# First attention: value products of two steps in one block behind a pair's denominators, with five probability slots and seven key slots

## The chip, the core and the metric

The kernel runs on one core of a Trainium2 chip. The core has five engines, each with its own queue, tied by semaphores only: TensorE (PE) multiplies matrices and writes into PSUM, VectorE (DVE) and ScalarE (ACT) read PSUM and work elementwise, GpSimd (POOL) works on SBUF alone, and SyncE (SP) issues most of the transfers. The metric is the device time of one execution in microseconds (us). Lower is better. All times here are for the whole program, of which the changed part is one stage.

## What is computed

The reference is a network of two layers on one sequence of 2048 tokens with 512 features, all in float32. Each layer has attention and a feed-forward part, with a residual and a layer norm behind each. The change touches the first attention alone:

```python
S, H, Dh = 2048, 16, 32
q = concat([x @ Wq_sem.T, rope(x @ Wq_geo.T)])    # 16 heads of 32
k = concat([x @ Wk_sem.T, rope(x @ Wk_geo.T)])
v = x @ Wv.T
scores = einsum('bhqd,bhkd->bhqk', q, k) / sqrt(32)
scores = where(causal, scores, float32.min)
attn = softmax(scores, axis=-1)
out = einsum('bhqk,bhkd->bhqd', attn, v)
x = layernorm(x + out @ Wo.T)
```

Behind it come a mixture of eight experts (two for each token) with a shared one, a second attention with 128-wide heads, and a gated feed-forward part with 2:4 sparsity. They aren't changed.

## The kernel before

**Items and steps.** The first attention (`layer0_attention`, from L478 on) works through 16 items: four chunks c of 512 queries (`CH`), and for each four groups g of four heads (`GH`). An item's keys are taken in tiles of 128; one step is one item with one key tile. Chunk c has 4c full tiles and four on the diagonal, so the items have 4, 8, 12 and 16 steps, 160 in all. For c > 0 full and diagonal tiles alternate as long as there are diagonal ones, then the remaining full ones follow. A diagonal step uses 512, 384, 256 or 128 of the queries. Two neighbouring steps are a pair; items have even numbers of steps, so no pair spans two items.

**What a step does.** For each of its four heads TensorE makes a *score* matmul (L726, 97 rows: 96 of split queries and keys and one that subtracts the row's maximum) into one of three banks `stb`, on the diagonal with a second one that adds the mask (L731). ScalarE makes the exponential of it (L619) into the step's slot of `probs`. Then follow the *value product* (`av`, L743: four matmuls, one for each head, with 32 columns of the array each, side by side, summed in `avb` over the item) and, once for each pair, the *denominators* (`den`, L759: four matmuls of the same shape with ones, summed in `den`). For the denominators GpSimd adds the second step's probabilities onto the first's, in place, in two halves of two heads (L590), and it may only do so when the value product of the first step is done. At the end of an item ScalarE copies `avb` (L633), VectorE turns the denominators and inverts them (L664, L668, L673: transpose, reciprocal, transpose), and GpSimd multiplies both into `X` (L600).

**The maxima.** The maximum that a score subtracts comes from a pass of its own, ahead of the item: *units* (L705), matmuls of queries with keys of up to 512 columns, into one of three banks `sbank`; VectorE takes the maximum of each (L645, on the diagonal L650), and at the item's end a *turn* (L657, L712, L626, L538, L540) brings the row of maxima to the queries. 640 units lie between the scores, about four for each step.

**What sets the order.** `attention0_plan` (L377 to L475) writes one list of events, and every engine goes through this same list in its own loop and picks its events: TensorE units, scores, `av` and `den`; GpSimd at an even `av` the pair's add (and, for the first 39 pairs, a transfer of zeros), and at the `den` of an item's last pair the multiply into `X`; VectorE at that `den` its three operations. `av` of step i-1 stands ahead of the last head's score of step i, and at odd i `den` of the pair i-3 stands behind it. Each engine's queue is worked off in this order, so whatever stands behind a waiting instruction waits too.

**Slots.** `probs` has four slots (`PSLOTS`), one a step: ScalarE may write slot i%4 when `av` and, by parity, `den` or the add of step i-4 is done. Keys are in eight slots (`KSLOTS`, parts of the buffers `hi` and `lo`), queries in three; SyncE loads 40 key chunks of three transfers each (L528) and may overwrite a slot when the last score that reads it is done.

Of the kernel before, what the change touches and what calls it, by code (L numbers as in the profile page):

```python
# [126 lines left out]
KSLOTS, QSLOTS, PSLOTS = 8, 3, 4  # L127
# [3 lines left out]
def key_slots(hi, lo):  # L131
    return [a[:, i, :].rearrange("p (h n) -> p h n", h=GH) for i, a in
            ((2, hi), (2, lo), (0, hi), (0, lo), (1, hi), (1, lo), (3, hi), (3, lo))]
# [243 lines left out]
def attention0_plan():  # L377
# [87 lines left out]
    for i, (n, kt) in enumerate(steps):  # L465
        for h in range(4):
            if h == 3 and i > 0:
                order.append(("av", i - 1))
                if i >= 3 and i % 2:
                    order.append(("den", i - 3))  # L470
            order.append(("scores", i, h))
            order += in_gap[k]
            k += 1
    order += [("av", len(steps) - 1), ("den", len(steps) - 2)]
# [3 lines left out]
def layer0_attention(nc, stage_before, qk_dram, m_dram, xs_dram, V, X, hi, lo, qst, consts, early):  # L478
# [14 lines left out]
    with ExitStack() as ctx:  # L493
# [3 lines left out]
        probs = m.sb("probs", [P, PSLOTS, GH, CH])  # L497
# [71 lines left out]
        def _(pool):  # L569
# [10 lines left out]
            for ev in order:  # L580
                if ev[0] == "av" and ev[1] % 2 == 0:
# [3 lines left out]
                    for a in range(2):  # L585
                        hs = slice(2 * a, 2 * a + 2)
                        pool.wait_ge(s["exp_ok"], 4 * (i + 1) + 2 * a + 2)
                        if a == 0:
                            pool.wait_ge(s["av_ok"], i + 1)
                        nc.gpsimd.tensor_tensor(probs[:, i % PSLOTS, hs, w0:], probs[:, i % PSLOTS, hs, w0:],  # L590
                                                probs[:, (i + 1) % PSLOTS, hs, w0:], ALU.add)\
                            .then_inc(s["pair_ok"], 1)
# [12 lines left out]
        def _(act):  # L605
            for ev in order:
                if ev[0] == "scores":
# [5 lines left out]
                    if i >= PSLOTS and h == 0:  # L613
                        act.wait_ge(s["av_ok"], i - PSLOTS + 1)
                        if i % 2 == 0:
                            act.wait_ge(s["den_ok"], (i - PSLOTS) // 2 + 1)
                        else:
                            act.wait_ge(s["pair_ok"], 2 * ((i - PSLOTS) // 2 + 1))
                    nc.scalar.activation(probs[:, i % PSLOTS, h, w0:], stb[:, k % 3, w0:], ACT.Exp, scale=SCALE0)\  # L619
# [58 lines left out]
        def _(pe):  # L678
# [12 lines left out]
            for ev in order:  # L691
# [41 lines left out]
                elif ev[0] == "av":  # L733
# [8 lines left out]
                    for h in range(GH):  # L742
                        last = nc.tensor.matmul(avb[HD0 * h:HD0 * (h + 1), w0:],  # L743
                                                V[:, kt, g * P + h * HD0:g * P + (h + 1) * HD0],
                                                probs[:, i % PSLOTS, h, w0:], start=start, stop=stop,
                                                tile_position=(0, HD0 * h), skip_group_check=True)
                    last.then_inc(s["av_ok"], 1)
                elif ev[0] == "den":
# [9 lines left out]
                    for h in range(GH):  # L758
                        last = nc.tensor.matmul(den[HD0 * h:HD0 * (h + 1), w0:], ones[:], probs[:, i % PSLOTS, h, w0:],  # L759
# [1445 lines left out]
def build(nc, ins, out):  # L2205
# [9 lines left out]
    with ExitStack() as ctx:  # L2215
# [20 lines left out]
        with ExitStack() as ffn:  # L2236
# [7 lines left out]
            with ExitStack() as both:  # L2244
                hi = both.enter_context(nc.sbuf_tensor("hi0", [P, ND, S], F32R))
                lo = both.enter_context(nc.sbuf_tensor("lo0", [P, ND, S], F32R))
# [3 lines left out]
                consts = (hidden, ident, identr, maskr)  # L2250
                stage = layer0_qkv(nc, ins["xT"], ins["wqk0"], ins["wv0"], ins["rope0"], ins["masks"], ins["eye"],
                                   X, V, hi, lo, qst, consts, qk0_dram)
                stage = layer0_attention(nc, stage, qk0_dram, m_dram, xs_dram, V, X, hi, lo, qst, consts, early)
# [108 lines left out]
```

## Time and profile before

| what | us |
|---|---|
| median of three runs | 2433.03 |
| lowest, highest | 2430.97, 2436.6 |
| profiled execution, its own time | 2435.74 |
| its span, first to last instruction | 2433.9 |
| first attention in it, first unit to last denominators | about 165 to 790 |

The stages follow one another, so the slices of the profile can be assigned: of 40 slices of 61 us the first attention fills those from the third to the thirteenth. Over the whole span TensorE is busy 91% of the time (2216.2 us), VectorE 51%, ScalarE 30%, GpSimd 27%, and the granted TensorE clock is 0.954 of its full value on average. How to read rows: a time is the start in us from the span's start, the next number the duration; `128x512` is partitions by elements of a row; x8 are eight neighbouring records of one kind in one row (the eight records of one `av` or `den` in float32 are four matmuls); the bracket is the idle time ahead and what ended it.

### The profile page before, as it was taken

What the parts mean: (1) busy time and instruction counts of PE and PEld (TensorE: products, weight loads), DVE (VectorE), ACT (ScalarE), POOL (GpSimd) and SP (SyncE); (2) the same over time, 40 slices, a digit from 0 to 9 for tenths busy, and PEclk for the clock granted to TensorE, in tenths of its full rate; (3) what the DMA queues carried; (4) which work ended last, traced back from release to release, by engine and by line L of the source; (5) the groups of instructions that cost most, each with busy time, mean ns of one, the idle gap of its engine ahead of it and who ended that gap; (6) DMA issues with size and microseconds to landing.
All of it is one profiled execution on the core that took longest, in us unless ns stands there. A gap on an engine that the chain in (4) does not pass through costs nothing. (4 is left out here: it accounts for less than half of the span.)

```text
span 2433.9 us, 27331 instructions
## 1 busy us (share of the span) xinstructions
PE 2216.2 (91%) x10140; PEld 1523.5 (63%) x10140; DVE 1244.0 (51%) x2244; ACT 734.5 (30%) x1318; POOL 663.5 (27%) x446
## 2 busy tenths in 40 slices
PE   7977999999998779999977877999999999999996
PEld 5864555455553544444446666888887787878775
DVE  6864577776660552222248872322224555455656
ACT  3322455555556332111123321211113221112222
POOL 5342455555556005110034633000003021211200
PEclk9976799999999889999998998999999999999999
DMA  4464244333210523232233425000011010100001
GB/s 176 173 179 120 82 117 128 106 87 79 66 27 19 210 94 138 74 113 78 83 122 129 137 106 190 27 18 27 18 35 44 9 35 18 35 17 17 18 18 52
DMA packets 102058, 196.07 MB, mean 81 GB/s; under 512 B 10080, under 2 KB 27360, under 8 KB 100512
## 3 DMA queue, kind: packets, MB, share of 16 engines
q1 hardware_dynamic: 92832, 164.29, 22.0%
q0 software_dynamic: 8240, 27.01, 3.2%
q10 hardware_dynamic: 864, 3.15, 0.4%
q8 instruction: 77, 1.26, 0.2%
q14 instruction: 45, 0.37, 0.0%
HBM read 127.69 MB, written 66.72 MB: 80 GB/s over the span
## 5 line engine op out<-in xcount | busy, mean ns | idle before, releaser
L619 ACT ACTIVATE a_probs<-a_stb 128x512 f32<-128x512 f32 (+3 forms) x640 | 308.8, 535 | 283.7 <-PE a_stb L731 168.8
L590 POOL TENSOR_TENSOR a_probs<-a_probs 128x1024 f32<-128x1024 f32 (+3 forms) x160 | 281.6, 1773 | 290.1 <-PE a_avb L743 275.1
L645 DVE TENSOR_REDUCE a_mparts<-a_sbank 128x1 f32<-128x512 f32 x384 | 239.8, 683 | 99.8 <-PE a_sbank L705 99.6
L2050 POOL CAST m_wh<-wst 128x1024 fp32r<-128x1024 f32 x24 | 27.6, 1148 | 727.4 <-POOLq L1811 373.6
L56 PE MATMUL m_gu<-hi,m_wh 128*128 128x512 f32 x512 | 202.4, 395 | 14.9 <-DVE m_h L2116 13.0
L57 PE MATMUL m_gu<-lo,m_wh 128*128 128x512 f32 x512 | 201.2, 393 | 0.0
L58 PE MATMUL m_gu<-hi,m_wl 128*128 128x512 f32 x512 | 201.1, 393 | 0.0
L650 DVE CUSTOM_DVE_ANT_0 a_junk<-a_sbank,hidden 128x128 bf16<-128x128 f32 (+3 forms) x256 | 113.8, 488 | 83.4 <-PE a_sbank L705 81.5
L743 PE MATMUL a_avb<-a_probs,V 128*32 128x512 f32 (+3 forms) x1280 | 155.6, 559 | 0.7 <-ACT a_probs L619 0.7
L705 PE MATMUL a_sbank<-hi,q 96*128 96x512 f32 (+3 forms) x320 | 134.6, 450 | 21.3 <-PEq L152 11.5
L2116 DVE TENSOR_TENSOR m_h<-m_sg,m_gu 128x512 f32<-128x512 f32 x64 | 43.9, 686 | 206.2 <-ACT m_sg L2080 206.1
L705 PE MATMUL a_sbank<-lo,q 96*128 96x512 f32 (+3 forms) x320 | 120.4, 412 | 17.6 <-DMA q<-qk 11.2
L726 PE MATMUL a_stb<-q,hi 97*128 97x512 f32 (+3 forms) x320 | 133.1, 427 | 1.5 <-ACT a_probs L619 1.3
L56 PE MATMUL a_sc<-hi,q 128*128 128x512 f32 x256 | 106.7, 417 | 19.1 <-PEq L1364 14.4
L726 PE MATMUL a_stb<-q,lo 97*128 97x512 f32 (+3 forms) x320 | 121.8, 392 | 1.6 <-ACT a_probs L619 1.2
L56 PEld LDWEIGHTS m_gu<-hi,m_wh 128*128 128x128 f32 x512 | 97.1, 190 | 37.6 <-DVE m_h L2116 15.6
L1895 DVE TENSOR_TENSOR a_ptl<-a_tb,a_pth 128x512 fp32r<-128x512 f32 x64 | 44.1, 691 | 149.2 <-ACT a_pth L1867 149.2
L2080 ACT ACTIVATE m_sg<-m_gu 128x512 f32<-128x512 f32 x64 | 38.3, 598 | 271.7 <-PE m_gu L58 248.8
L1867 ACT ACTIVATE a_pth<-a_tb 128x512 fp32r<-128x512 f32 x64 | 38.2, 598 | 243.0 <-PE a_tb L1935 243.0
L58 PEld LDWEIGHTS m_gu<-hi,m_wl 128*128 128x128 f32 x512 | 97.3, 190 | 20.7
L57 PEld LDWEIGHTS m_gu<-lo,m_wh 128*128 128x128 f32 x512 | 97.4, 190 | 20.2
L726 PEld LDWEIGHTS a_stb<-q,hi 97*128 97x128 f32 x320 | 62.7, 198 | 68.2 <-ACT a_probs L619 33.9
(256 smaller groups left out, 4765.9 us busy)
## 6 DMA issues: line engine op xcount, KB each, us to landing
qk<-v_hl SPq DMA_DIRECT2D x32, 512.0 KB, 2.7
hi<-qk SPq DMA_DIRECT2D x60, 256.0 KB, 4.8
lo<-qk SPq DMA_DIRECT2D x60, 256.0 KB, 5.6
q<-qk SPq DMA_DIRECT2D x48, 256.0 KB, 5.3
wst<-in_w_mlp SPq DMA_DIRECT2D x24, 512.0 KB, 3.5
xs<-a_zeros POOLq DMA_DIRECT2D x39, 256.0 KB, 2.5
w<-xs SPq DMA_DIRECT2D x39, 256.0 KB, 2.8
ys<-e_rows_b SPq DMA_DIRECT2D x39, 256.0 KB, 2.0
```

The lines of the kernel that those rows point to most:

```text
L56: nc.tensor.matmul(out, wh, xh, start=start, stop=False, skip_group_check=True)
L57: nc.tensor.matmul(out, wh, xl, start=False, stop=False, skip_group_check=True)
L58: return nc.tensor.matmul(out, wl, xh, start=False, stop=stop, skip_group_check=True)
L590: nc.gpsimd.tensor_tensor(probs[:, i % PSLOTS, hs, w0:], probs[:, i % PSLOTS, hs, w0:], probs[:, (i + 1) % PSLOTS, hs, w0:], ALU.add)\
L619: nc.scalar.activation(probs[:, i % PSLOTS, h, w0:], stb[:, k % 3, w0:], ACT.Exp, scale=SCALE0)\
L645: nc.vector.reduce_max(to, sbank[:, b, :], AX).then_inc(s["unit_max"], 1)
L650: nc.vector.tensor_tensor_reduce(out=junk[:, k % 2, 0:w], in0=sbank[:, b, 0:w], in1=hidden[:, CH - w:CH], scale=1.0, scalar=BIG, op0=ALU.a ...
L705: nc.tensor.matmul(bank[:, 0:w], qst[0:96, n % QSLOTS, h, t * P:(t + 1) * P], kst[at % KSLOTS][0:96, h, 0:w], start=True, stop=True)\
L726: last = nc.tensor.matmul(stb[:, k % 3, w0:], kst[slot_of[n, kt // TC] % KSLOTS][0:97, h, kt % TC * P:(kt % TC + 1) * P], qst[0:97, n % QS ...
L743: last = nc.tensor.matmul(avb[HD0 * h:HD0 * (h + 1), w0:], V[:, kt, g * P + h * HD0:g * P + (h + 1) * HD0], probs[:, i % PSLOTS, h, w0:], ...
L1895: nc.vector.tensor_tensor(ptl[:, 4 * g:4 * g + 4, :].rearrange("p a b -> p (a b)"), tb[:, (g + 1) % 2, :], f32(pth[:, 4 * g:4 * g + 4, :]) ...
L2116: tt(h[:, r, :], sg[:], gu[:, r % 2, 1, :], ALU.mult).then_inc(s["h_ok"], 1)
```

## The change

The list of events is written in another order. At odd i nothing stands between the scores any more. At even i, ahead of the last head's score, stand: `den` of the pair i-4, `av` of i-2, `av` of i-1, in this order. The end of the list is `den`, `av`, `av`, `den`. Since a step's probabilities are needed for longer, there is a fifth slot: `several` has four and `spare` is placed on the memory of the eighth key slot, so `KSLOTS` is 7. The waits of ScalarE, which go by the parity of i - 4, go by that of i - 5. Nothing else is changed: as many matmuls, adds, exponentials and transfers as before, one memset fewer.

```diff
-KSLOTS, QSLOTS, PSLOTS = 8, 3, 4
+KSLOTS, QSLOTS, PSLOTS = 7, 3, 5
...
-            ((2, hi), (2, lo), (0, hi), (0, lo), (1, hi), (1, lo), (3, hi), (3, lo))]
+            ((2, hi), (2, lo), (0, hi), (0, lo), (1, hi), (1, lo), (3, hi))]
...
         for h in range(4):
-            if h == 3 and i > 0:
-                order.append(("av", i - 1))
-                if i >= 3 and i % 2:
-                    order.append(("den", i - 3))
+            if h == 3 and i > 0 and i % 2 == 0:
+                if i >= 4:
+                    order.append(("den", i - 4))
+                order += [("av", i - 2), ("av", i - 1)]
             order.append(("scores", i, h))
             order += in_gap[k]
             k += 1
-    order += [("av", len(steps) - 1), ("den", len(steps) - 2)]
+    n = len(steps)
+    order += [("den", n - 4), ("av", n - 2), ("av", n - 1), ("den", n - 2)]
...
-        probs = m.sb("probs", [P, PSLOTS, GH, CH])
+        several = m.sb("probs", [P, PSLOTS - 1, GH, CH])
+        probs = [several[:, i] for i in range(PSLOTS - 1)] + [spare[:]]
...
                     if i >= PSLOTS and h == 0:
                         act.wait_ge(s["av_ok"], i - PSLOTS + 1)
-                        if i % 2 == 0:
+                        if (i - PSLOTS) % 2 == 0:
                             act.wait_ge(s["den_ok"], (i - PSLOTS) // 2 + 1)
                         else:
                             act.wait_ge(s["pair_ok"], 2 * ((i - PSLOTS) // 2 + 1))
...
+                lo_at = (nc.sbuf_base + 31) // 32 * 32
...
+                spare = nc.alloc_sbuf_tensor_at("spare0", [P, GH, CH], F32, offset=lo_at + 4 * 3 * S)
```

On TensorE, at the end of the last item's narrow steps (around its eighth step; `a_stb` are scores, `a_avb` a value product, `a_den` denominators). Before:

```order
L726 MATMUL a_stb<-q,lo 128x512 x3
L743 MATMUL a_avb<-a_probs,V 32x128 x4
L726 MATMUL a_stb<-q,lo 128x512 x4
L743 MATMUL a_avb<-a_probs,V 32x512 x4
L759 MATMUL a_den<-a_probs,a_ones 32x512 x4
L726 MATMUL a_stb<-q,lo 128x512 x4
```

The same place now:

```order
L728 MATMUL a_stb<-q,hi 128x512 x3
L761 MATMUL a_den<-a_probs,a_ones 32x512 x4
L745 MATMUL a_avb<-a_probs,V 32x512 x4
L745 MATMUL a_avb<-a_probs,V 32x128 x4
L728 MATMUL a_stb<-q,hi 128x512 x8
```

The value products left their places between four scores each; two stand together, behind the denominators, and eight scores of 512 columns follow in a row.

On GpSimd, from the last narrow pair of the second last item to the first pairs of the last one (`a_probs<-a_probs` is a pair's add, x2 its halves; `X` the multiply). Before:

```order
L590 TENSOR_TENSOR a_probs<-a_probs 128x2x128 x2
L590 TENSOR_TENSOR a_probs<-a_probs 128x1024 x10
L600 TENSOR_TENSOR X<-a_avs,a_rt 128x512
L590 TENSOR_TENSOR a_probs<-a_probs 128x2x384 x2
```

The same place now:

```order
L592 TENSOR_TENSOR spare_57<-spare_57,a_probs 128x2x128 x2
L592 TENSOR_TENSOR a_probs<-a_probs 128x1024 x2
L592 TENSOR_TENSOR a_probs<-a_probs,spare_57 128x1024 x2
L592 TENSOR_TENSOR a_probs<-a_probs 128x1024 x4
L602 TENSOR_TENSOR X<-a_avs,a_rt 128x512
L592 TENSOR_TENSOR spare_57<-spare_57,a_probs 128x1024 x2
L592 TENSOR_TENSOR a_probs<-a_probs 128x2x384 x2
```

Between the narrow pair and the multiply stood five full adds (x10), now four; the fifth, the first of the new item, moved behind the multiply.

## Rows read from the trace of the kernel before

**Rows 1.** Windows, core 0: stretch, length, busy us of each engine, PEclk, DMA share, GB/s.

```profile
300.00:734.00 434.00, 422.49 (x2616) 223.74 (x2610) 303.39 (x705) 243.19 (x503) 242.35 (x161) 1.00 0.34 86
```

**Rows 2.** Waits of PE, 190 to 790 us: us in total, times, longest.

```profile
PE a_sbank L705 <- DVE a_mparts L645: 7.5, 18, 1.1
```

**Rows 3.** Timeline of PE and DVE, 601 to 605 us: start, us, engine, line, operation.

```profile
601.25 0.39 PE L705 MATMUL a_sbank<-hi,q 96*128 96x512 f32 x1
601.57 1.07 PE L743 MATMUL a_avb<-a_probs,V 128*32 128x512 f32 x8
602.45 1.04 PE L759 MATMUL a_den<-a_probs,a_ones 128*32 128x512 f32 x8
603.42 0.50 PE L726 MATMUL a_stb<-q,lo 97*128 97x512 f32 x1
603.76 0.40 PE L705 MATMUL a_sbank<-hi,q 96*128 96x512 f32 x1
603.99 0.40 PE L726 MATMUL a_stb<-q,lo 97*128 97x512 f32 x1
...
604.19 2.49 DVE L645 TENSOR_REDUCE a_mparts<-a_sbank 128x1 f32<-128x512 f32 x4 [1.43 <-PE a_sbank L705]
```

**Rows 4.** Timelines of PE and ACT, 733 to 790 us, without units in between.

```profile
733.96 1.06 PE L743 MATMUL a_avb<-a_probs,V 128*32 128x512 f32 x8
734.96 0.97 PE L726 MATMUL a_stb<-q,hi 97*128 97x512 f32 x3
...
767.02 0.98 PE L726 MATMUL a_stb<-q,lo 97*128 97x512 f32 x3
767.56 2.07 ACT L619 ACTIVATE a_probs<-a_stb 128x512 f32<-128x512 f32 x4 [1.41 <-PE a_stb L726]
768.21 0.50 PE L726 MATMUL a_stb<-q,lo 97*128 97x512 f32 x1 [0.21 <-ACT a_probs L619]
...
780.80 1.07 PE L743 MATMUL a_avb<-a_probs,V 128*32 128x512 f32 x8
...
789.37 1.07 PE L759 MATMUL a_den<-a_probs,a_ones 128*32 128x512 f32 x8 [1.86 <-POOL a_probs L590]
```

**Rows 5.** Timeline of PE, POOL and DVE around an item's final denominators, 688 to 693 us.

```profile
688.22 1.06 PE L743 MATMUL a_avb<-a_probs,V 128*32 128x512 f32 x8
689.11 1.04 PE L759 MATMUL a_den<-a_probs,a_ones 128*32 128x512 f32 x8
689.47 4.70 POOL L590 TENSOR_TENSOR a_probs<-a_probs 128x1024 f32<-128x1024 f32 x2 [2.60 <-PE a_avb L743]
690.21 0.72 DVE L664 STREAM_TRANSPOSE a_dt<-a_den 128x512 f32<-128x512 f32 x1 [1.14 <-PE a_den L759]
691.25 0.71 DVE L673 STREAM_TRANSPOSE a_rt<-a_rec 128x512 f32<-128x512 f32 x1
691.89 2.44 DVE L645 TENSOR_REDUCE a_mparts<-a_sbank 128x1 f32<-128x512 f32 x4
692.60 0.50 PE L705 MATMUL a_sbank<-lo,q 96*128 96x512 f32 x1 [0.50 <-DVE a_mparts L645]
```

**Rows 6.** Groups of POOL by form, 190 to 790 us: xcount, busy us, mean ns.

```profile
L590 POOL TENSOR_TENSOR a_probs<-a_probs 128x768 f32<-128x768 f32 x32 | 57.9, 1828 | 86.4 <-PE a_avb L743 86.2 <-ACT a_probs L619 0.2
L600 POOL TENSOR_TENSOR X<-a_avs,a_rt 128x512 f32<-128x512 f32 x15 | 19.3, 1290 | 0.2
```

**Rows 7.** Timeline of PE, 225 to 240 us.

```profile
231.27 9.55 PE L705 MATMUL a_sbank<-hi,q 96*128 96x512 f32 x16 [5.26 <-DMA q<-qk]
```

**Rows 8.** Later stage: two waits in PE's timeline, and the window behind the first.

```profile
1909.40 0.50 PE L56 MATMUL m_gu<-hi,m_wh 128*128 128x512 f32 x1 [2.73 <-DVE m_h L2116]
...
2045.67 0.50 PE L56 MATMUL m_gu<-hi,m_wh 128*128 128x512 f32 x1 [2.02 <-DVE m_h L2116]
...
1910.80:1914.20 3.40, 3.40 (x10) 2.66 (x9) 1.53 (x3) 0.00 (x0) 0.00 (x0) 0.52 0.00 0
```

**Rows 9.** Key loads of L528, from issue to landing.

```profile
DMA to landing us min/median/max: 3.2/4.9/8.6
```

More of the change, by code:

```diff
@@ L473, in attention0_plan, with layer0_attention @@
             k += 1
-    order += [("av", len(steps) - 1), ("den", len(steps) - 2)]
+    n = len(steps)
+    order += [("den", n - 4), ("av", n - 2), ("av", n - 1), ("den", n - 2)]
     return items, steps, first, final, units, loads, last_use, order
-def layer0_attention(nc, stage_before, qk_dram, m_dram, xs_dram, V, X, hi, lo, qst, consts, early):
+def layer0_attention(nc, stage_before, qk_dram, m_dram, xs_dram, V, X, hi, lo, qst, consts, early, spare):
     items, steps, first, final, units, loads, last_use, order = attention0_plan()
@@ L589, in _ @@
                             pool.wait_ge(s["av_ok"], i + 1)
-                        nc.gpsimd.tensor_tensor(probs[:, i % PSLOTS, hs, w0:], probs[:, i % PSLOTS, hs, w0:],
-                                                probs[:, (i + 1) % PSLOTS, hs, w0:], ALU.add)\
+                        nc.gpsimd.tensor_tensor(probs[i % PSLOTS][:, hs, w0:], probs[i % PSLOTS][:, hs, w0:],
+                                                probs[(i + 1) % PSLOTS][:, hs, w0:], ALU.add)\
                             .then_inc(s["pair_ok"], 1)
@@ L618, in _ @@
                             act.wait_ge(s["pair_ok"], 2 * ((i - PSLOTS) // 2 + 1))
-                    nc.scalar.activation(probs[:, i % PSLOTS, h, w0:], stb[:, k % 3, w0:], ACT.Exp, scale=SCALE0)\
+                    nc.scalar.activation(probs[i % PSLOTS][:, h, w0:], stb[:, k % 3, w0:], ACT.Exp, scale=SCALE0)\
                         .then_inc(s["exp_ok"], 1)
@@ L744, in _ @@
                                                 V[:, kt, g * P + h * HD0:g * P + (h + 1) * HD0],
-                                                probs[:, i % PSLOTS, h, w0:], start=start, stop=stop,
+                                                probs[i % PSLOTS][:, h, w0:], start=start, stop=stop,
                                                 tile_position=(0, HD0 * h), skip_group_check=True)
@@ L758, in _ @@
                     for h in range(GH):
-                        last = nc.tensor.matmul(den[HD0 * h:HD0 * (h + 1), w0:], ones[:], probs[:, i % PSLOTS, h, w0:],
+                        last = nc.tensor.matmul(den[HD0 * h:HD0 * (h + 1), w0:], ones[:], probs[i % PSLOTS][:, h, w0:],
                                                 start=start, stop=stop, tile_position=(0, HD0 * h),
@@ L2250, in build @@
                 consts = (hidden, ident, identr, maskr)
+                spare = nc.alloc_sbuf_tensor_at("spare0", [P, GH, CH], F32, offset=lo_at + 4 * 3 * S)
                 stage = layer0_qkv(nc, ins["xT"], ins["wqk0"], ins["wv0"], ins["rope0"], ins["masks"], ins["eye"],
                                    X, V, hi, lo, qst, consts, qk0_dram)
-                stage = layer0_attention(nc, stage, qk0_dram, m_dram, xs_dram, V, X, hi, lo, qst, consts, early)
+                stage = layer0_attention(nc, stage, qk0_dram, m_dram, xs_dram, V, X, hi, lo, qst, consts, early, spare)
             xt = V[:].rearrange("p (d c) n -> p d (c n)", d=ND)
```

## The prediction

> **What bounds the kernel now.** I read the windows first, to find the stage that the change touches and which engine is full in it. From 300 to 734 us TensorE is busy 97% of the time at a granted clock of 1.00, VectorE 70%, ScalarE 56%, GpSimd 56% [rows 1]. Then the table of waits of TensorE in this stage (190 to 790 us): the largest that recurs is 18 waits of 7.5 us in all, for VectorE's maxima [rows 2]. So the stage goes by TensorE's own sequence; a change there counts in full, and a new wait on TensorE counts in full too. Then the timeline of one pair of steps, for what the sequence costs. Value and denominator matmuls use 32 columns of the array at four tile positions, the others all 128. Two neighbours of the 32-column kind start 0.88 us apart, neighbours of the full kind 0.23. At a border it is more: 0.32 from the last full one to the value product, 0.34 from the first full one to the next, and 0.97 from the denominators to the first full one [rows 3]; 1.00 where a value product stands alone [rows 4]. So a value product that stands alone pays (0.32 - 0.23) + (1.00 - 0.88) + (0.34 - 0.23) = 0.32 us for its borders. Last, the timeline around a final denominator, for the chain that hangs on GpSimd [rows 5], whose durations are in the table by form [rows 6].
>
> **What the change removes.** 160 blocks of 32-column work become 80 (the order shows all of it: block, four heads' products, block). 80 borders of 0.32 us are 25.6 us. Nine of them lie in the last 55 us, which I sum apart, and some three before 231 us, where TensorE waits 5.26 us for a query load [rows 7] and gives nothing back. 68 x 0.32 = **-21.8 us**. VectorE's three small operations after a final denominator run now behind the first scores of the next stretch, where the third or fourth unit waits 0.50 us for them [rows 5]; they will run beside a block of 2.7 us. I take half of the 7.5 us of [rows 2]: **-4 us**.
>
> **What it adds: GpSimd before the block.** The pair's add of the block at T starts when that block's first value product is done, and must have ended when the next block starts, since that now begins with the pair's denominators. A value product starts and 1.25 us later the add does (688.22 to 689.47), which takes 4.70 us for two full halves [rows 5]. The denominators stand first, so the next block is at T + 0.88 + 1.25 + 4.70 + 0.05 = T + 6.9 at the earliest (0.05 as where a score follows the end of the exponential that it waits for, 767.56 + 0.60 and 768.21 [rows 4]). The pair of steps is three products of 0.88, a way out of 0.09 and a stretch of eight scores and seven or eight units, 3.9 to 4.2: 6.6 to 6.9. So plain pairs just fit, for **+1 us** in all. Before, the denominators came last in their block, 0.88 us later.
>
> **The final pairs don't fit.** In the order of GpSimd the multiply into X now stands ahead of the next item's first add (it was behind it). The multiply needs three VectorE operations on the denominators: the first starts 1.10 us after these (689.11 to 690.21), the last ends at 691.96, 2.85 after them [rows 5]. VectorE has its last units to finish at that point, so I add 0.2. The multiply takes 1.29 [rows 6]. Only then the add: T + 3.05 + 1.29 + 4.70 + 0.05 = **T + 9.1**. What TensorE has in these places is 6.85 (2.73 in the block, about 4.1 in the stretch, which has a diagonal step with its mask matmuls). So it stands still for 2.25 us, ahead of denominators that all the rest of its work is queued behind, scores and units included; ScalarE and VectorE run dry with it. There are 15 such places. One lies in the tail, two in the first 260 us are covered by the query load and by TensorE at half its clock. 12 x 2.25 = **+27 us**. The bounds: 1.7 us where the stretch has more in it, 2.6 where VectorE is later.
>
> **Longer stretches on three banks.** VectorE takes a full unit each 0.60 us (four in 2.49, the last 0.69) and starts 0.43 after the matmul [rows 3]; TensorE goes on 0.71 after the start of the maximum that it waits for (691.89 is the first, the wait ends at 692.60 [rows 5], and the bank is the one of three before). In a stretch of four units nothing waits. In one of eight, unit j starts at 0.34 + 0.467j unhindered, and can't before 1.48 + 0.60(j - 3): at j = 7 that is 3.88 against 3.61, 0.27 us late; with a ninth unit early in the stretch 0.63. Of some 15 such stretches ten are of the first kind or have mask matmuls between, five of the second: 10 x 0.3 + 5 x 0.63 = **+6 us** (3 to 9). ScalarE keeps up: one exponential per 0.49 us.
>
> **The tail.** Once the units are over (from 733.96), eight pairs of steps take 46.8 us until 780.80, and the last denominators start 8.57 later [rows 4]. The scores of a stretch are then paced by ScalarE: the fourth waits until the first exponential has ended (1.19 after the first score), the rest follow by 0.49 ((2.06 - 0.60)/3 of [rows 4]), so eight scores and the way into the block are 1.19 + 4 x 0.49 + 0.4 = 3.6, where two stretches of four took 3.2. By the chains: four plain full pairs at 6.9, one final at 9.1, and three with narrower diagonal steps: 5.8 (the add is two of 1.83 [rows 6]: 0.88 + 1.25 + 3.66), 5.0 by TensorE and 5.6 by ScalarE. That is 53.1, **+6.3 us**. At the end two full chains follow one another, 2 x 6.9 = 13.8 instead of 8.57, less the 2.06 us by which a block now starts earlier (a denominator and a value product that it no longer has behind it, and a border): **+3.2 us**.
>
> **The clock.** In the later stages, at full clock too, seven waits of TensorE of 1.9 to 2.7 us stand in the trace; after three of them the granted clock fell: behind one of 2.73 us the row shows 0.52 over 3.4 us, which is 1.2 of 2.4 GHz nearly throughout; after one of 2.02 us nothing fell [rows 8]. Each fall costs half of its length, 1.7 us. 13 waits of 2.25 us and more (the 12 and the tail's one) x 3/7 x 1.7 = **+9.5 us** (0 to 35, if the falls are longer and come at each). The Trainium skill ("TensorE: Matmul & The Clock Gate", "Why this matters for your kernels") only warns of pauses longer than the ones forecast here. By it this term would be nil; the rows say otherwise, and the rows decide.
>
> **Key slots, loads.** Seven slots instead of eight don't move a single unit or score in the order. The tightest load is freed ten scores ahead of its first use, with a block between: 10 x 0.47 + 2.7 = 7.4 us and more. Its three transfers are issued 0.43 apart and land 4.9 after that (median; 8.6 at most [rows 9]): about 6.2. Nothing, or some 2 us in one place. A memset less is nothing.
>
> **Sum** against the profiled execution's 2435.74: -21.8 - 4 + 1 + 27 + 6 + 6.3 + 3.2 + 9.5 = **+27.2 us**. The median of the runs shown is 2433.03, so **2460**.
>
> **Rivals.**
> - *No fall of the clock.* All as above without the last term: 2433 + 18 = 2451. For it: four of seven such waits left the clock alone. 0.27.
> - *The clock falls at each stall and in the tail*, where TensorE is then idle a third of each pair: 13 x 1.7 = 22 instead of 9.5, 8 more in the tail, where slower value products also delay the adds that hang on them, and some falls of twice the length: 2433 + 18 + 22 + 8 + 5 = 2486. 0.14.
> - *Faster: GpSimd isn't last.* If the add of the first pair didn't wait behind the multiply, the final pairs would be at 6.9 as well and TensorE's borders would be what is left: -21.8 - 4 + 1 + 6 + 2 = -17, 2416. It decides at T + 6.9: an add that ends before that costs nothing. Against it stands the order of GpSimd, in which the multiply comes first, and that the engine works in order. 0.08.
> - *Partly covered.* Stalls of 1 us less and short rings: -12 -3, so near +3 us, 2436. 0.07.
> - *Late keys.* The load of 6.2 us against 7.4 lands late at a dozen places by 1 us: 2472. 0.04.
> - *That it doesn't do what it says*: the blocks are halved in the order, but a value product next to another one might pay a load that one next to denominators doesn't. 80 x 0.2 more: 2476. 0.02.
> The forecast itself has 0.38.
>
> **The numbers.** Below 2440 lie the faster case and the partly covered one, 0.15; above 2490 a part of the clock's case. A range from 2438 to 2488 holds the rest. A measurement of this kernel can tell about 0.2%, 4.9 us, from no change. Faster: 0.08 and a third of the partly covered: 0.09. Within: 0.07. Slower: 0.84.
>
> **What the profile after would show.** Right: 80 blocks; the multiply into X ahead of an add; about 13 waits of TensorE for GpSimd's adds of about 2 us, each right after a final denominator's block and ahead of the next denominators, and short ones in the last 50 us; VectorE waits on its units about 0.3 us at the end of long stretches; the clock below 1.00 somewhere between 300 and 790. Wrong: if the table of waits has no such row the final pairs' term falls and the kernel is faster; if the borders inside a block are over 0.9 the first term does.

## The result, and the profile after

| | before | after |
|---|---|---|
| median of four runs, us | 2432.70 | 2452.05 |
| lowest to highest | 2430.97 to 2436.60 | 2448.17 to 2456.19 |
| span of the profiled execution | 2433.9 | 2454.4 |
| mean granted clock | 0.954 | 0.950 |
| last denominators of the first attention | 789.37 | 806.25 |

The changed kernel takes 1.0075 times as long (95% interval 1.0062 to 1.0089); the medians differ by 19.4 us. Of the 20.5 us between the two spans 16.9 stand at the last denominators. Nearly all of the other 3.6 came up in two steps of 1.6 us in the last stage of the network, which the change doesn't touch: 24.4 us at half clock there against 17.8. I count them as scatter, which was not tested. Of ten executions of the run `both`, further down, one took 3157.7 us at a mean granted clock of 0.648; its times here are those of the other nine.

Lines of functions are two higher in the kernel after: L707 are units, L728 scores, L745 value products, L761 denominators, L592 GpSimd's adds, L602 its multiply into X. The same window and the waits of TensorE (190 to 805 us), to be held against [rows 1, 2]:

```profile
300.00:734.00 434.00, 407.93 (x2519) 220.77 (x2518) 291.27 (x680) 236.17 (x486) 232.58 (x155) 0.97 0.33 85
...
PE a_den L761 <- POOL a_probs L592: 24.0, 17, 2.5
PE a_sbank L707 <- DMA q<-qk: 9.6, 3, 6.8
PE a_den L761 <- POOL spare L592: 8.6, 5, 3.1
PE a_sbank L707 <- DVE a_mparts L647: 3.8, 15, 0.3
```

TensorE's busy share fell from 97% to 94%, its clock from 1.00 to 0.97, and a row that was nearly absent (one wait of 1.9 us) is now the largest: 32.6 us of waits for GpSimd's adds in 22 places, and one of 4.0 at 806 us outside this window. The waits for maxima went down to half.

A fixed amount of work is the fairest comparison. From the sixth turn to the last one both kernels run 2641 matmul records of this stage. Windows of before and of after:

```profile
294.33:733.52 439.19, 427.36 (x2641) 226.12 (x2642) 307.70 (x712) 245.54 (x509) 243.76 (x163) 1.00 0.33 86
```

```profile
279.96:736.52 456.56, 427.77 (x2641) 231.01 (x2641) 304.51 (x712) 246.91 (x509) 245.90 (x165) 0.97 0.32 85
```

So the middle became 17.4 us longer. But the sixth turn comes 14.4 us *earlier* than before, which I had not forecast, and from the last turn to the last denominators it takes 69.7 us instead of 55.9. 16 matmul records, two products or 1.8 us, moved from before the sixth turn to behind the last one. Without them the start gained 12.6 us, the middle lost 17.4 and the tail 12.1: together the 16.9.

**A final pair after.** Timeline of PE, DVE and POOL in the tail, where nothing else covers the wait:

```profile
752.21 1.07 PE L761 MATMUL a_den<-a_probs,a_ones 128*32 128x512 f32 x8 [0.43 <-POOL a_probs L592]
...
753.35 0.72 DVE L666 STREAM_TRANSPOSE a_dt<-a_den 128x512 f32<-128x512 f32 x1 [16.88 <-PE a_den L761]
...
754.39 0.71 DVE L675 STREAM_TRANSPOSE a_rt<-a_rec 128x512 f32<-128x512 f32 x1
...
755.24 1.27 POOL L602 TENSOR_TENSOR X<-a_avs,a_rt 128x512 f32<-128x512 f32 x1 [3.08 <-DVE a_rt L675]
...
756.47 4.67 POOL L592 TENSOR_TENSOR spare<-spare,a_probs 128x1024 f32<-128x1024 f32 x2
...
761.20 1.08 PE L761 MATMUL a_den<-spare,a_ones 128*32 128x512 f32 x4 [3.06 <-POOL spare L592]
```

The next denominators start 761.20 - 752.21 = 8.99 us later, with the multiply ahead of the add. The forecast was T + 9.1. In the middle the same wait stands at each final pair, 0.7 to 2.4 us long: the largest are 2.31, 2.32 and 2.37 at 583, 642 and 702 us. During one of them, 0.9 us before it ends, the clock falls; the wait and a window that begins there:

```profile
641.98 1.93 PE L761 MATMUL a_den<-a_probs,a_ones 128*32 128x512 f32 x8 [2.32 <-POOL a_probs L592]
```

```profile
641.20:644.60 3.40, 2.62 (x16) 0.65 (x20) 0.00 (x0) 0.00 (x0) 0.73 (x1) 0.50 0.00 0
```

0.50 is 1.2 of 2.4 GHz. By windows of 0.5 us laid side by side TensorE is at this level for 30.6 us between 300 and 805 us; in the kernel before it never is between 300 us and its last denominators.

**The end.** The last two blocks of PE:

```profile
799.46 1.06 PE L761 MATMUL a_den<-a_probs,a_ones 128*32 128x512 f32 x8 [1.95 <-POOL a_probs L592]
...
806.25 1.94 PE L761 MATMUL a_den<-a_probs,a_ones 128*32 128x512 f32 x8 [4.01 <-POOL a_probs L592]
```

### The profile page after: what moved, and what is told of

It reads as the page before. It is cut to its first block and busy times, and to the rows that moved or that the text cites. A ratio compares the mean times of both kernels' runs of the same rounds, so it can differ in the third digit from the quotient of the medians.

```text
span 2454.4 us, 27325 instructions
## 1 busy us (share of the span) xinstructions
PE 2216.8 (90%) x10140; PEld 1530.7 (62%) x10140; DVE 1241.4 (51%) x2244; ACT 735.0 (30%) x1318; POOL 659.7 (27%) x445
## 3 DMA queue, kind: packets, MB, share of 16 engines
q1 hardware_dynamic: 92832, 164.29, 21.8%
## 5 line engine op out<-in xcount | busy, mean ns | idle before, releaser
L621 ACT ACTIVATE a_probs<-a_stb 128x512 f32<-128x512 f32 (+3 forms) x512 | 249.5, 538 | 202.3 <-PE a_stb L728 161.6
L2052 POOL CAST m_wh<-wst 128x1024 fp32r<-128x1024 f32 x24 | 27.8, 1156 | 729.3 <-POOLq L1813 372.5
L592 POOL TENSOR_TENSOR a_probs<-a_probs 128x1024 f32<-128x1024 f32 (+3 forms) x96 | 167.9, 1768 | 134.7 <-PE a_avb L745 134.7
L707 PE MATMUL a_sbank<-hi,q 96*128 96x512 f32 (+3 forms) x368 | 145.2, 428 | 15.5 <-PEq L152 11.4
L728 PE MATMUL a_stb<-q,hi 97*128 97x512 f32 (+3 forms) x368 | 139.8, 393 | 1.7 <-ACT a_probs L621 1.2
L707 PE MATMUL a_sbank<-lo,q 96*128 96x512 f32 (+3 forms) x272 | 114.1, 448 | 10.2 <-DMA q<-qk 9.3
L745 PE MATMUL a_avb<-a_probs,V 128*32 128x512 f32 (+3 forms) x1024 | 117.9, 570 | 0.0
L728 PE MATMUL a_stb<-q,lo 97*128 97x512 f32 (+3 forms) x272 | 109.0, 413 | 0.7 <-ACT a_probs L621 0.4
L707 PEld LDWEIGHTS a_sbank<-hi,q 96*128 96x128 f32 x368 | 73.0, 203 | 52.9 <-DVE a_mparts L647 23.3
```

The lines of the kernel that those rows point to most:

```text
L592: nc.gpsimd.tensor_tensor(probs[i % PSLOTS][:, hs, w0:], probs[i % PSLOTS][:, hs, w0:], probs[(i + 1) % PSLOTS][:, hs, w0:], ALU.add)\
L621: nc.scalar.activation(probs[i % PSLOTS][:, h, w0:], stb[:, k % 3, w0:], ACT.Exp, scale=SCALE0)\
L707: nc.tensor.matmul(bank[:, 0:w], qst[0:96, n % QSLOTS, h, t * P:(t + 1) * P], kst[at % KSLOTS][0:96, h, 0:w], start=True, stop=True)\
L728: last = nc.tensor.matmul(stb[:, k % 3, w0:], kst[slot_of[n, kt // TC] % KSLOTS][0:97, h, kt % TC * P:(kt % TC + 1) * P], qst[0:97, n % QS ...
L745: last = nc.tensor.matmul(avb[HD0 * h:HD0 * (h + 1), w0:], V[:, kt, g * P + h * HD0:g * P + (h + 1) * HD0], probs[i % PSLOTS][:, h, w0:], ...
```

## The experiments

All times in us. "6th", "12th" and "last" are the starts of TensorE's turns in the profiled execution, "end" is the last denominators; the ratio is against runs of the kernel before on the same chip.

| kernel | 6th | 12th | last | end | median | ratio, 95% interval |
|---|---|---|---|---|---|---|
| before | 294.3 | 508.8 | 733.5 | 789.4 | 2433 | 1 |
| after | 280.0 | 504.9 | 736.5 | 806.3 | 2452.1 | 1.0075 (1.0062 to 1.0089) |
| x_behind | 279.3 | 488.5 | 705.2 | 772.0 | 2420.6 | 0.9952 (0.9935 to 0.9968) |
| x_ahead | 298.3 | 516.8 | 745.3 | 806.4 | 2457.5 | 1.0107 (1.0079 to 1.0136) |
| keys7 | 286.7 | 502.7 | 727.4 | 783.3 | 2429.0 | 0.9983 (0.9974 to 0.9993) |
| den_last | 282.3 | 500.3 | 719.8 | 779.9 | 2425.4 | 0.9966 (0.9953 to 0.9978) |
| tail_single | 279.6 | 488.4 | 705.2 | 766.4 | 2414.6 | 0.9924 (0.991 to 0.9937) |
| q_early | 286.7 | 502.6 | 727.3 | 783.2 | 2428.2 | 0.9974 (0.9963 to 0.9985) |
| before_half | 286.4 | 496.9 | 718.1 | 774.0 | 2419.4 | 0.994 (0.9925 to 0.9955) |
| behind_half | 279.0 | 482.6 | 693.4 | 759.6 | 2402.3 | 0.9866 (0.9851 to 0.9881) |
| x_vector | 282.2 | 512.4 | 733.7 | 793.5 | 2436.0 | 1.001 (1.0 to 1.002) |
| q_first | 275.9 | 482.8 | 713.2 | 773.1 | 2421.9 | 0.9951 (0.9934 to 0.9967) |
| both | 277.9 | 495.9 | 729.0 | 790.3 | 2431.6 | 0.9999 (0.9988 to 1.001) |
| q_part | 274.9 | 481.6 | 698.6 | 758.5 | 2406.0 | 0.9887 (0.987 to 0.9903) |

The theory was the prediction's: the grouping saves borders, and GpSimd's order at the final pairs costs more than that. The rival was that the grouping itself, by its chains, rings or slots, is what is slow.

### x_behind: the changed kernel with the multiply moved behind the next add

```diff
+                    for n in ready:
+                        multiply(n)
+                    ready.clear()
                 elif ev[0] == "den" and ev[1] + 1 in final:
-                    ...
-                    nc.gpsimd.tensor_tensor(X[:, c * NG + g, :], ...)
+                    ready.append(steps[ev[1]][0])
```

> The changed kernel, with one thing altered on GpSimd: the multiply of an item's result into X stands behind the add of the next item's first pair, as it did before the change. Theory (GpSimd's queue at the final denominators): TensorE's waits for GpSimd's adds were 32.6 us in 22 places in the changed kernel; the 13 of about 2 us behind final denominators go, the short ones of 0.5 in the last 50 us and the last of 4.0 stay: 32.6 becomes 8 to 10. With the falls of the clock that followed some of them: 2452 becomes 2420 to 2430. Rival (the long blocks cost by themselves, through the maxima's banks or the clock): the waits move to other rows and the time stays above 2442.

2420.6: inside the expectation, as are the waits for adds, 9.5 us in all. Its window from the sixth turn to the last, and the waits for adds in it:

```profile
279.32:705.18 425.86, 416.29 (x2640) 228.80 (x2641) 304.19 (x712) 246.75 (x509) 245.56 (x165) 1.00 0.35 91
...
PE a_den L769 <- POOL a_probs L600: 0.5, 3, 0.2
```

Against after, one instruction's place in GpSimd's queue is worth 456.56 - 425.86 = 30.7 us in the middle. In after the waits for adds in this stretch are 19.1 us, here 0.5; the half-clock time is 27.2 us in after and 3.4 here, worth half the difference, 11.9. Together 30.5 of the 30.7. And the grouping without the stall is a gain: 13.3 us against before, in the same work.

### x_ahead: the kernel before with the multiply ahead of the next add

```diff
+            mine = list(order)
+            for at, ev in enumerate(order[:-1]):
+                after = order[at + 1]
+                if ev[0] == "av" and after[0] == "den" and after[1] + 1 in final and ev[1] % 2 == 0:
+                    mine[at], mine[at + 1] = after, ev
-            for ev in order:
+            for ev in mine:
```

> The kernel before, with only GpSimd's order altered: the multiply into X stands ahead of the next item's first add, as in the changed kernel; TensorE's order, slots and loads are those of before. Theory: the pair of steps behind a final denominator can't be shorter than 9.1 us, where it has 7.1 to 8.0 now (6.0 in the last item): 1 to 2 us in some 12 places and 3 in the last item, 15 to 27 us in all, with a few falls of the clock: 2450 to 2465, and a row of waits of TensorE for the adds of 15 to 25 us. Rival (the order on GpSimd doesn't matter without the long blocks): 2433 within 4.

2457.5, inside the expectation, so the place of the multiply alone makes the old grouping slower too. The four runs lie between 2451 and 2463; the profiled one is among the quicker, and its trace accounts for 17 of the 24 us. In the middle it is milder: 446.98 against 439.19 us, with these waits, and one late in the stage:

```profile
PE a_den L764 <- POOL a_probs L595: 4.6, 6, 0.8
...
699.91 1.04 PE L764 MATMUL a_den<-a_probs,a_ones 128*32 128x512 f32 x8
708.90 1.06 PE L764 MATMUL a_den<-a_probs,a_ones 128*32 128x512 f32 x8 [0.78 <-POOL a_probs L595]
```

From final denominators to the next ones it is 708.90 - 699.91 = 8.99 us, to the hundredth the chain of the changed kernel. But in the old order TensorE has 8.0 us of work between the two (before: 689.11 to 697.15), since the next denominators stand at the end of their block, behind more scores and units and two single value products. In the new order it has 6.9 (x_behind: 665.42 to 672.31). The same chain costs 0.8 us there and 2.1 to 2.4 here. I had expected 1 to 2 us in some 12 places; it is 0.7 to 0.8 in six. The remaining 9 us of the 17 come at the start (4.0) and in the tail (5.3), with waits of 2.3 to 2.7 us at narrow steps, so the total came out right in part by luck.

### keys7 and q_early: where the early gain comes from

keys7 is the kernel before with seven key slots; q_early keeps eight and changes SyncE's order by hand:

```diff
-KSLOTS, QSLOTS, PSLOTS = 8, 3, 4
+KSLOTS, QSLOTS, PSLOTS = 7, 3, 4
```

```diff
+            work.sort()
+            at = [w[2:4] for w in work].index(("q", 3))
+            while work[at - 1][2] == "k":
+                work[at - 1], work[at] = work[at], work[at - 1]
+                at -= 1
```

> The kernel before with seven key slots instead of eight and nothing else. Theory from the trace of the changed kernel: a key load for which there is no slot yet is issued behind the query load that TensorE waits for at 197 us, so that wait shrinks from 11.2 to 7 us and the later stretch at half the clock gets shorter: 2418 to 2427. The prediction's own view (the loads have room either way): 2433 within 4.

> The kernel before, with one edit: on SyncE's queue the query load of the fourth item stands ahead of the two key loads that it stood behind. Eight key slots as before. Theory (the seven slots helped the start only because they let a query load pass ahead of a key load): the load is issued 3 us earlier, TensorE's wait for it falls from 11.2 us to 7 to 9, the half-clock time around 228 to 270 us falls with it, the median is 2426 to 2431 us. Rival (the order of the two loads doesn't matter, fewer key loads in flight do): the wait and the median stay, 2431 to 2436.

Both put the sixth turn at 286.7 instead of 294.3, within 0.02 us of each other, and the end at 783.2 and 783.3. By the medians they gain 4.5 and 5.5 us; the 7.7 us at the sixth turn are between single executions, and the profiled one of the kernel before is itself 2.7 us above its median. The 2429.0 of keys7 missed my 2418 to 2427, the 2428.2 of q_early is inside its range. So my view that slots cost nothing was wrong, and since q_early has all eight slots, the order of the queue is enough to bring the gain about. SyncE's timeline before, and in keys7:

```profile
195.54 1.26 SPq L528 DMA_DIRECT2D hi<-qk  x3
196.84 1.59 SPq L528 DMA_DIRECT2D lo<-qk  x3
198.48 1.72 SPq L534 DMA_DIRECT2D q<-qk  x3
```

```profile
194.08 1.42 SPq L528 DMA_DIRECT2D hi<-qk  x3
195.54 1.85 SPq L534 DMA_DIRECT2D q<-qk  x3
197.44 1.78 SPq L528 DMA_DIRECT2D hi<-qk  x3
```

With one slot less a key load becomes possible later, so the query load that TensorE waits for passes it and is issued 3 us earlier. In q_early it isn't issued earlier (198.97 us, since there it waits for its own slot), against my expectation; but with no key load ahead of it its last part lands 7.0 us after the issue instead of 10.0. The waits for query loads shrink by less than the gain (17.4 us before, 16.8 in keys7, 13.2 in q_early). What shrinks more is the time at half clock behind them: between 190 and 300 us it is 61.5 us before, 41.0 in keys7, 42.7 in q_early. Half of the difference, 9 to 10 us, is more than the whole gain of 7.7. A caution: the run before_half, below, leaves the loads in their old order and its sixth turn comes at 286.4 too, with 42 us at half clock. So another cause can shorten that stretch as well; how the order of the loads does it is not resolved.

### den_last: the changed kernel with the denominators behind the value products

```diff
-                if i >= 4:
-                    order.append(("den", i - 4))
                 order += [("av", i - 2), ("av", i - 1)]
+                if i >= 4:
+                    order.append(("den", i - 4))
```

> The changed kernel with the denominators at the end of the block instead of at its beginning (value product, value product, denominators); GpSimd then has an add ahead of the multiply into X as before. Theory (the chain through GpSimd is what cost): an add has 1.8 us more, so neither final nor plain pairs wait, the pairs of the last item go by ScalarE at 6.3 us, and the end is as before: waits for GpSimd below 4 us, 2410 to 2420. Rival (long blocks cost by themselves): above 2435.

2425.4, a clear gain over after but outside my range, and 4.8 us behind x_behind. The waits for adds are gone from the middle, as expected; in the tail 5.1 us stay, where I had said below 4, and the tail is 6.7 us shorter than that of x_behind. What I had left out are VectorE's three operations on a final `den`. They now come after the block, in front of the maxima of the next stretch, as before the change: 13 of the 23 waits for maxima of the middle, 6.6 of 9.0 us, stand within 6 us behind the first of them, against 3 waits and 0.8 us in x_behind. Waits of PE, den_last from 282.33 to 553.21 us, and x_behind over the same work, 279.32 to 540.38:

```profile
PE a_sbank L707 <- DVE a_mparts L647: 5.9, 16, 1.0
```

```profile
PE a_sbank L715 <- DVE a_mparts L655: 2.4, 10, 0.3
```

The two stretches differ by 9.8 us. Waits for maxima, those of diagonal units included, are 4.3 of it and waits for query loads 1.0. The other 4.5 lie inside TensorE's busy time; 1.7 of them are one more fall of the clock, the rest is not resolved.

### before_half and behind_half: VectorE's pace in long stretches

```diff
-                        nc.vector.reduce_max(to, sbank[:, b, :], AX)
+                        nc.vector.reduce_max(to, sbank[:, b, 0:CH // 2], AX)
```

> The kernel before, with VectorE's maximum of a full unit read over 256 of its 512 columns (so the row maxima are those of half the keys: part of the work is left out). It takes VectorE's pace away. Theory: TensorE's 20 waits for maxima (9.3 us) go, the last three items fall from 170.1 us together to 167 to 168, the median is 2424 to 2428 us. Rival (TensorE isn't held by VectorE): 2431 to 2435.

> The same left out (maxima over 256 of 512 columns) in the run x_behind, to see how much VectorE's pace of 0.60 us a unit costs in the long stretches, where it shows in no wait. Theory (a pair of blocks grouped saves 8 borders of 0.32 us an item, of which the pace of VectorE gives 0.8 back): an item of the last three falls from 54.9 us to 54.0 to 54.5, no lower because full pairs then meet GpSimd's chain at 6.9 us, with waits of 0.1 to 0.3 us for adds; against before_half the item is 1.5 to 2.0 us shorter, or 2.5 with these waits taken off. Rival (a border is worth 0.23 us and the pace costs nothing): the item stays at 54.6 to 54.9 and no new waits for adds show.

The prediction charged 6 us for banks that VectorE frees too late, but waits for maxima went down in after. The windows over the last three items, 24 pairs, show where that term is: before, before_half, x_behind, behind_half.

```profile
563.40:733.52 170.12, 166.39 (x1011) 86.25 (x1012) 116.18 (x252) 97.29 (x199) 97.48 (x52) 1.00 0.22 52
```

```profile
550.41:718.11 167.70, 165.23 (x1011) 86.45 (x1011) 86.13 (x252) 97.23 (x199) 97.53 (x52) 1.00 0.22 53
```

```profile
540.38:705.18 164.80, 161.03 (x1010) 87.25 (x1011) 114.43 (x252) 96.46 (x198) 97.27 (x51) 1.00 0.24 59
```

```profile
531.97:693.42 161.45, 157.68 (x1011) 88.98 (x1012) 86.71 (x252) 95.79 (x198) 97.30 (x51) 1.00 0.25 60
```

With VectorE quick, grouping takes 165.23 - 157.68 = 7.55 us of TensorE's busy time, 0.31 for each of 24 pairs: the border of 0.32 us. With VectorE as it is, the same grouping takes only 166.39 - 161.03 = 5.36, or 0.22. So VectorE's pace takes 2.2 us back in three items, and it stands in *busy* time. Over all 61 pairs from the sixth turn to the last, reckoned in the same way, grouping takes 423.71 - 405.86 = 17.9 us of busy time with VectorE quick, and 427.36 - 416.29 = 11.1 with VectorE as it is. With half of each run's half-clock time taken off (1.7, 3.4, 0 and 1.7 us) that is 19.6, or 0.32 for each pair, and 12.8: an estimate of 6.8 us taken back. In elapsed time less of it is seen in the last three items, 6.25 against 5.32 us gained, because in behind_half waits for adds of 1.0 us come in. The timeline of PE in a long stretch of after shows how:

```profile
601.23 0.41 PE L707 MATMUL a_sbank<-hi,q 96*128 96x512 f32 x1
601.47 0.40 PE L728 MATMUL a_stb<-q,hi 97*128 97x512 f32 x1
601.73 0.50 PE L707 MATMUL a_sbank<-hi,q 96*128 96x512 f32 x1
602.07 0.40 PE L728 MATMUL a_stb<-q,hi 97*128 97x512 f32 x1
602.33 0.50 PE L707 MATMUL a_sbank<-hi,q 96*128 96x512 f32 x1
```

Units follow each other by 0.60 us here at the end, VectorE's pace, instead of 0.47; the unit starts a few hundredths late and the next score 0.34 behind it, and no idle time is noted. The item of behind_half, 53.8 us, is a little below my 54.0 to 54.5, and small waits for adds did appear, six of 0.2 us: with VectorE out of the way GpSimd's chain is next. The last three items of before_half, 167.7 us, are as expected. Not all of its waits for maxima went: 11 of 20 stay, 5.2 of 9.3 us. Its median, 2419.4, is some 5 us below my 2424 to 2428; I had counted nothing for the start, where the sixth turn came 7.9 us earlier.

### tail_single: x_behind with the last item in single blocks

```diff
+            if i > first[-1]:
+                if h == 3:
+                    order.append(("av", i - 1))
+                    if i % 2:
+                        order.append(("den", i - 3))
-            if h == 3 and i > 0 and i % 2 == 0:
+            elif h == 3 and i > 0 and i % 2 == 0:
```

> The changed kernel with the multiply into X behind the next pair's add, as in the run x_behind, and the last item (16 steps, after the last scores of which no units are left) in the single blocks of the kernel before. The last item took 55.9 us from the last turn to the last denominators in the kernel before, 66.9 us in x_behind. Theory (the grouping itself costs the tail: eight scores are paced by ScalarE, the chain of GpSimd is last): this stretch takes 56 to 58 us, the median comes to 2409 to 2414 us. Rival (the tail is long for the fifth probability slot's waits or for the clock, not for the grouping): the stretch stays above 63 us and the median within 2417 to 2424.

From the last turn to the end: 61.2 us, against 66.9 in x_behind and 55.9 before; I had said 56 to 58. I had forgotten the 1.8 us of products that the grouping had moved behind the last turn; another 1.7 are one fall of the clock (3.4 us from 711.8 on). Without these it is 57.7. The median, 2414.6, is just above my range and 6.0 below that of x_behind, and the rival is out: the fifth slot is still there. In the tail the grouping itself is what costs; of the 5.7 us between the two tails 1.7 are a second fall of the clock in x_behind.

### x_vector, q_first, both: two edits that should have helped

x_vector gives the multiply to VectorE (the same operation, `nc.vector.tensor_tensor`, behind the last transpose). q_first lets each query load pass the key loads right before it:

```diff
+            for m in range(EARLY, NI):
+                at = [w[2:4] for w in work].index(("q", m))
+                while work[at - 1][2] == "k":
+                    work[at - 1], work[at] = work[at], work[at - 1]
+                    at -= 1
```

> As tail_single, but the multiply into X is VectorE's, right behind its last transpose, so that GpSimd has the pair adds alone. Theory (all that is left of the final pairs' stall is GpSimd's queue): the waits for adds behind final denominators (0.2 to 0.5 us each, 1.29 us once in the last item) go, the maxima behind the multiply come 0.6 us later at 16 places, half of it seen by TensorE: 2411 to 2417 us. Rival (VectorE has less to spare than GpSimd: half of the maxima's work was worth 14 us in before_half): the middle stretch from the sixth turn to the last grows by 5 us or more, the median is 2418 or more.

> As tail_single, with each query load of SyncE's queue moved ahead of the key loads right before it. Theory (q_early's gain, 5.5 us in the kernel before, came from the order alone, and seven slots gave about the same; here one key load stands ahead of the first query load and up to two ahead of later ones): TensorE's waits for query loads fall from 15.0 us to 9 to 12, the median to 2409 to 2413 us. Rival (the loads wait for their slot, not for the queue): waits and median stay, 2413 to 2417; or a key load now comes late and it is slower.

> The edits of x_vector and q_first together on tail_single. If they act in different places, the median differs from that of tail_single by the sum of their two differences, within 3 us; 2407 to 2414 us. If VectorE is what holds the start as well, where the loads come first, less than the sum.

All three missed by their medians. **x_vector** is 21 us slower than tail_single, and the rival, which I had priced at 5 or more, is right by far. The multiply takes VectorE 0.69 us at the end of the stage, where GpSimd is idle. It takes 2.0 us (median of 16) elsewhere. In the timeline:

```profile
638.98 5.16 POOL L596 TENSOR_TENSOR a_probs<-a_probs 128x1024 f32<-128x1024 f32 x2 [2.39 <-PE a_avb L747]
...
639.86 2.05 DVE L678 TENSOR_TENSOR X<-a_avs,a_rt 128x512 f32<-128x512 f32 x1
...
796.53 0.69 DVE L678 TENSOR_TENSOR X<-a_avs,a_rt 128x512 f32<-128x512 f32 x1
```

GpSimd's first add began 0.88 us ahead of the multiply and lasts 2.38. The multiply ends at 641.91, that is 0.55 behind that add's end at 641.36. It is so in all 15 places where an add is under way when the multiply starts: the multiply, itself 0.7 us long, ends 0.54 to 0.56 behind that add, however long it has waited. The second add then takes 2.82 instead of 2.38, so the pair of adds has 5.16 instead of some 4.7. So the two don't share, they wait for each other. The Trainium skill ("SBUF — State Buffer", "SBUF: two separate sides") says the same: a VectorE operation with two inputs in SBUF and a GpSimd operation that reads SBUF take a common pair of ports as an exclusive lock, for the whole instruction. Behind the multiply the maxima are late: TensorE's waits for them from the sixth turn to the last are 13.6 us in 23 places instead of 3.2 in 13, and the clock was at half for 30.6 us instead of 3.4. That is 10.4 + 13.6 = 24.0 of the 25.8 us by which this stretch is longer.

**q_first** has its waits for query loads down to 10.4 us, as expected. It won at the start (12th turn at 482.8 instead of 488.4) and lost 13.5 us behind it. Waits of PE from 480 to 720 us, and the longest of them:

```profile
PE a_sbank L729 <- DMA lo<-qk: 7.2, 3, 3.7
```

```profile
511.70 0.80 PE L729 MATMUL a_sbank<-lo,q 96*128 96x512 f32 x1 [3.73 <-DMA lo<-qk]
```

These are key loads that had been passed. With 13.6 us at half clock behind them they make 7.2 + 6.8 = 14.0. **both** has both losses: 17.0 us over tail_single, where the two single differences add up to 28.7, so they overlap in part; where, was not resolved.

### q_part: query loads first in the first twelve items only

> As q_first, but only the query loads of the first twelve items pass ahead of the key loads; those of the last four items stay in the place that they have in tail_single. Theory (q_first was quicker by 5.6 us at the twelfth turn, 482.8 against 488.4, and lost 13.5 after it because key loads that had been passed came up to 3.7 us late in the items with four key loads each): turns as in q_first up to the twelfth, from there intervals of 54.9 us as in tail_single, median 2407 to 2412 us. Rival (the loss comes from the clock or from elsewhere): the intervals after the twelfth stay at 58 and the median near 2422.

2406.0 us, just below the expected range, 0.9887 of the kernel before: 27.8 us faster than it and 46 faster than the change as it was made. The last three intervals are 55.2, 55.0 and 55.0 us as in tail_single, and no wait for a key load is left, so the loss of q_first was the late keys, with the falls of the clock behind them. What is left of waits for query loads:

```profile
PE a_sbank L729 <- DMA q<-qk: 9.1, 4, 3.8
```

## Why the prediction was right, and where it was not

The time was 2452 for a forecast of 2460, and 20.5 us between the profiles for a sum of 27.2. Step by step:

- **Borders, -21.8 - 4.** Right. The price of a border is 0.31 us measured in busy time (before_half against behind_half) for 0.32. The waits for maxima fell from 9.3 us to 3.8 (the 7.5 of my rows leave out two at diagonal units), 5.5 us for 4, and den_last, in which VectorE's three operations have no block beside them, got part of them back.
- **Plain pairs, +1.** Right: full blocks in the tail follow by 785.78 to 792.63 = 6.85 us, and in the middle no plain pair waits for an add. How close it is shows in x_behind, where the final pairs have the plain chain: three waits of 0.2 us.
- **Final pairs, +27.** The chain was right (8.99 to 9.12 for 9.1; 9.36 and 9.90 at two places where VectorE came later), the stall too large: eleven waits in the middle make 19.1 us, 1.7 each, not 2.25. Three more, 5.5 us together, stand ahead of the sixth turn. The step that was off is the "6.85 that TensorE has in these places": it is 6.7 us in the last three items, where the waits are 2.3, but in items of fewer steps the stretch can hold more. At 451.68 us it is 8.4 with eleven units instead of seven, and the wait is 0.74.
- **Long stretches, +6.** Right, though I looked for it in the wrong view. It is 2.2 us in the last three items and 6.8 over the middle, and not one row of the waits shows it.
- **Tail, +6.3 + 3.2.** 12.1 us longer without the products that moved there, of which 3.4 are two falls of the clock: 8.7 for 9.5. The last block waits 4.01 us for its add, as two full chains in a row make it.
- **Clock, +9.5.** Too small: from 300 to 800 us a fall stands at five of nine waits of 1.8 us or more for adds, where I took three of seven (the trace of the kernel before has at least one more such wait, 1.97 us at 1279, with a fall, which makes it four of eight), and some falls lasted 6.8 us instead of 3.4: 30.6 us at half clock from 300 to 805 us cost 15.3. One of them, 6.8 us long, stands at a wait of 2.44 us for a query load, which is in no term of the sum. Falls stand at or behind pauses as short as 1.81 us from 300 us on, 1.24 at 282.89, and in the tail 0.50 (743.82); in x_vector they stand behind waits for maxima of 0.7 to 1.4 us. The warning of the Trainium skill ("TensorE: Matmul & The Clock Gate", "Why this matters for your kernels"), by which this term would have been nil, is too narrow for this trace.
- **Key slots, 0.** This step failed. I asked only whether a load might come too late, not which loads stand behind it in SyncE's queue. Put alone into the kernel before, seven slots make the sixth turn 7.7 us earlier in the profile, and the whole 4.5 by the medians. The start gained 12.6; the rest, 4.9 us or more, I can't assign, the grouping and the clock are both in it.

So the forecast held because errors of both signs met: too much for the stalls and nothing for the start's gain, too little for the clock. That the total came within 8 us is luck; that it is slower, and by which chain, is not. Of the rivals, "faster, GpSimd isn't last" was the right one to fear: it is the run x_behind, which the order of one instruction separates from the change, and 2416 was its price for a measured 2420.6. That it is so close is partly luck as well: the price has nothing for the start, which gained, and next to nothing for the tail, which lost 9 us.

## What to carry to other kernels

Before work is moved past an event that several engines follow, list for each engine what changes places with what: here one multiply of 1.3 us that came to stand ahead of a 4.7 us add turned a gain of 12 us into a loss of 19, with the falls of the clock that came with its waits. The same holds for a transfer queue; a buffer slot fewer is also another order of loads. And a bound can hide in busy time: compare the time for the same count of instructions, not only the table of waits.

## What the runs showed of the hardware

- Two-input elementwise work of VectorE against adds of GpSimd, all on SBUF: 0.69 us alone, 2.0 in company (median of 16), for 512 elements a row; in 15 of 15 places it ends 0.54 to 0.56 us behind the add that was under way, and the next add is 0.4 us longer (x_vector).
- Of eight waits of TensorE for adds between 1.8 and 2.4 us, from 300 to 800 us in after, four have 3.4 or 6.8 us at half clock at or behind them; those of 1.91, 1.94, 1.95 and 1.99 us have none. But falls stand behind shorter waits too (0.50 in after, 0.7 to 1.4 in x_vector), so the length of a single pause doesn't tell.
- Units that another engine holds back by 0.13 us (0.60 apart for 0.47) show as busy time of TensorE, not as a wait: the records of neighbouring matmuls, 0.40 us long and 0.23 apart, overlap.
